# Attention and a routed expert layer in one kernel: the router's top logit carried in the row and applied after the expert gather, one table set per stage, a native fp32 router, shared-expert work inside the attention drain

## The chip, the cores and the metric

The kernel runs on one core of one Trainium2 chip. The metric is device time in microseconds (us) from launch to end. "Chunk" below is four row tiles of 128 tokens, 512 tokens; there are 32 tiles and 8 chunks. Engines: PE is TensorE (PEld its weight loads), DVE is VectorE, ACT ScalarE, POOL GpSimd, SP SyncE, which here only issues transfers.

## The reference

4096 tokens of 128 features pass through two residual blocks. Cut to what matters:

```python
def _L0_attn_ref(x, Wq, bq, Wk, bk, Wv, bv, Wo, bo, m):     # 16 heads of 8
    q = _l2norm(proj(Wq, bq)); k = _l2norm(proj(Wk, bk)); v = proj(Wv, bv)
    attn = jnp.einsum('bhid,bhjd->bhij', q, k) / n ** sigmoid(m)     # no softmax
    return jnp.einsum('bhij,bhjd->bhid', attn, v) ... @ Wo + bo

def _L0_ffn_ref(...):                                       # 16 experts, top 1
    logits = hidden @ router_w.T
    scores = sigmoid(top value, -inf elsewhere)
    routed_in = hidden[None, :, :] * scores.T[:, :, None]
    gate_up = einsum('nth,nhf->ntf', routed_in, gate_up_proj)
    routed_out = einsum('ntf,nfh->nth', up * silu(gate), down_proj)
    shared = silu(hidden @ shared_gate_w.T) * (hidden @ shared_up_w.T) @ shared_down_w.T

x = x + _L0_attn_ref(_layernorm(x), ...)
x = x + _L0_ffn_ref(_layernorm(x), ...)
```

## The kernel before

Each engine has one queue, and the order in it is the order in which the code is written for that engine; semaphores couple the five queues. There is no planner. Four stages follow one another.

**Attention.** Since there is no softmax, attention is q times (k'v), and `Wo` is folded into k'v. A loop over steps `s` works on several chunks at once. `project(s)` on PE makes q, k, v of chunk s; `take_qkv` on DVE scales and adds biases; `square` (ACT), `head_sums` (DVE), `head_norms` (ACT), `inv_norms` (DVE) and `scale_heads` (POOL) normalise the heads; `v_by_k`, `turn_q`, `fold_wo`, `attend` (PE) finish. `add_attn` (DVE, line 691) adds attention's output to the residual, `norm_h` (ACT) makes the second norm in `h_rows`, `turn_h` (PE) transposes it, `hT_hi` (ACT) and `hT_lo` (POOL) split it into two fp32r parts.

**Routing.** `route` multiplies with the router in three fp32r products per tile. `choose` (DVE) finds the expert of each token, `rank_tokens` (PE) counts, `place` (DVE) works out each token's row in a table `x_slots` in device memory, and `scatter` (POOL, line 397) writes the rows there by indirect transfers, 32 of them of 128 rows. Ahead of that, `score_rows` (ACT, lines 502 and 507) takes the sigmoid of the top logit and scales the row. After the last chunk SP fills the end of each expert's rows with zeros (16 transfers, line 300) and only then loads rows back.

**Windows.** 47 windows of 128 rows, in 12 groups of four, each window with the weights of one expert. `load_windows(q)` (SP, line 305) brings group q into `h_rows`; eight groups fit, so group q + 8 is loaded once group q's result has been stored:

```python
            for q in range(NG):
                sp.wait_ge(yg_rdy, q + 1)
                ...   # store yg
                if q + NQ < NG:
                    sp.wait_ge(gT_mm, q + 1)
                    load_windows(q + NQ)
```

`over_windows` sets the order on PE, ACT and DVE alike: in turn k `turn_x(k + 2)`, `gate_up(k)`, `turn_act(k - 1)`, `down(k - 2)`. On ACT these are `x_hi` (line 591), `silu_experts` (line 598), nothing, and `take_y` (line 608), which raises `yg_rdy`.

**Shared expert.** Chunks 0 and 1 (`gate_up_shared`, `down_shared`, lines 972 to 974 with `sgT`, `suT`, and 1009 to 1011) run before the windows, chunks 2 to 7 after them, beside 32 indirect gathers on POOL (line 424) that keep two transfers in flight.

Of the kernel before, what the change touches and what calls it, by code (L numbers as in the profile page):

```python
# [14 lines left out]
P = 128  # L15


def build_block(nc, x, xt, Wq, bq, Wk, bk, Wv, bv, Wo, bo, m, router_t, gate_up, down, gate_t, up_t, down_t, out):
# [16 lines left out]
    CAP = T + P  # L35
    QKV = 3 * D
# [6 lines left out]
    LATE = 2  # L43
# [3 lines left out]
    x_slots = nc.dram_tensor("x_slots", (E * CAP + SPARE * P, D), F32, kind="Internal").ap()  # L47
# [4 lines left out]
    with ExitStack() as ctx:  # L52
# [7 lines left out]
        h_rows = sb("h_rows", [P, NT, D])  # L60
# [17 lines left out]
        zero_rows = sb("zero_rows", [P, D])  # L78
        rwT = sb("rwT", [P, 2, E], F32R)
# [7 lines left out]
        top = sb("top", [P, NT])  # L87
        score = sb("score", [P, NT])
# [15 lines left out]
        win_no = sb("win_no", [1, NG * Q, E])  # L104
        win_start = sb("win_start", [1, NG * Q])
        past_n = sb("past_n", [1, NG * Q])
        past_jump = sb("past_jump", [1, NG * Q])
        win_e = sb("win_e", [1, NG * Q], I32)
        win_row = sb("win_row", [1, NG * Q], I32)
        gpos = sb("gpos", [P, NT], I32)  # L110

        with ExitStack() as attention:
            def sb_a(name, shape, dt=F32):
                return attention.enter_context(nc.sbuf_tensor(name, shape, dt))

# [28 lines left out]
        past = sb("past", [1, NG * Q, E])  # L144
        move = sb("move", [P, NT, E])
        moved = sb("moved", [P, NT])
        s_spl = sb("s_spl", [P, 2, 2, 512], F32R)
        yT = sb("yT", [P, 512])
        xgT = sb("xgT", [P, 2, 2, Q * P], F32R)
# [9 lines left out]
        ps_yT, ps_y = bank[0], bank[1]  # L159
        ps_gT, ps_aT, ps_yg = bank[3], bank[1], bank[2]  # L160
# [5 lines left out]
        ld_b, ld_wo, ld_wa = sem("ld_b"), sem("ld_wo"), sem("ld_wa")  # L166
# [11 lines left out]
        ssum, nrm, rn_rdy = sem("ssum"), sem("nrm"), sem("rn_rdy")  # L178
# [6 lines left out]
        top_rdy, log_read, score_rdy, hs_rdy = sem("top_rdy"), sem("log_read"), sem("score_rdy"), sem("hs_rdy")  # L185
        hot_rdy, rank_mm, rank_read, pos_rdy = sem("hot_rdy"), sem("rank_mm"), sem("rank_read"), sem("pos_rdy")
        scat = sem("scat")
# [4 lines left out]
        xg_ld = [sem(f"xg_ld{r}") for r in range(NQ)]  # L192
        gT_mm, gT_hi, gT_sb = sem("gT_mm"), sem("gT_hi"), sem("gT_sb")
# [11 lines left out]
        STEPS = NQ + 3  # L205
# [4 lines left out]

        def attended(s):

            return [c for c in range(NQ) if min(c + 3, NQ + 1) == s]

        def turned(s):

            return [c for c in range(NQ) if min(c + 4, NQ + 2) == s]

        def placed(s):

            return [c for c in range(NQ - LATE) if c + 5 == s]

        late = range(NQ - LATE, NQ)

# [4 lines left out]
        def rank_cols(c):  # L229

            at = ps_log[:, 256 + 80 * (c - late[0]):] if c in late else pair[:, 3, QKV:]
            return at[:, 0:(1 + Q) * E].rearrange("p (j e) -> p j e", e=E)
# [12 lines left out]
        def window_rows(q, engine):  # L245

            return table(win_row[0:1, Q * q:Q * q + Q], engine, E * CAP + (SPARE - 1) * P)

        def window_experts(q, engine):

            return table(win_e[0:1, Q * q:Q * q + Q], engine, (E - 1) * D)

        def over_windows(turn_x, gate_up, turn_act, down, filler):

            turn_x(0)
            turn_x(1)
            for k in range(NG + 2):
                if k + 2 < NG:
                    turn_x(k + 2)
                if k < NG:  # L260
                    gate_up(k)
                if 0 <= k - 1 < NG:
                    turn_act(k - 1)
                if 0 <= k - 2 < NG:
                    down(k - 2)
                if k >= NG:
                    filler(k - NG)
# [3 lines left out]
        def _(sp):  # L271
            for c in range(NQ):
# [6 lines left out]
                if c == 1:  # L279
                    sp.dma_start(bo_in[:], bo.partition_broadcast(2)).then_inc(ld_wo, 16)  # L280
# [13 lines left out]
            sp.dma_start(spare, zero_rows[:].unsqueeze(1).broadcast_to([P, SPARE, D])).then_inc(zero_st, 16)  # L294
# [7 lines left out]
            def load_windows(q):  # L302
                rows = window_rows(q, mybir.EngineType.SP)
# [6 lines left out]
            sp.wait_ge(scat, 16 * NT)  # L310
# [17 lines left out]
        def _(pool):  # L328
# [8 lines left out]
            g.memset(bo_pick[:, 1:2], 0.0)  # L337
            g.memset(zero_rows[:], 0.0).then_inc(k_set, 1)
# [20 lines left out]
            g.iota(base[:, 0, :], pattern=[[CAP, E]], base=0, channel_multiplier=0,  # L359
                   allow_small_or_imprecise_dtypes=True)  # L360
            g.iota(win_no[:], pattern=[[1, NG * Q], [0, E]], base=0, channel_multiplier=0,
                   allow_small_or_imprecise_dtypes=True)
            g.memset(hot[:, :, 0, :].bitcast(F32), 0.0)
            g.iota(win_start[:], pattern=[[P, NG * Q]], base=0, channel_multiplier=0,
                   allow_small_or_imprecise_dtypes=True).then_inc(k_ids, 1)

            def scale_heads(c, col, r_col, done):
# [3 lines left out]
                r = rn[:, c % 2, :, r_col:r_col + HEADS].unsqueeze(3).broadcast_to([P, Q, HEADS, HD])  # L371
# [13 lines left out]
            def weights_lo(n):  # L385
                w, raw = ((sgT, sg_in[:]), (suT, su_in[:]), (sdT, sd_in[:].rearrange("p k d -> p (k d)")),
                          (rwT, rw_in[:]))[n]
# [3 lines left out]
            def scatter(c, half):  # L391

                if half == 0:
                    pool.wait_ge(pos_rdy, c + 1)
                    pool.wait_ge(hs_rdy, c + 1)
# [754 lines left out]
```

## Time and profile before

| what | value |
|---|---|
| time, median of three runs | 272.96 us (272.4 to 273.98) |
| the profiled execution's own time | 275.04 us |
| its span | 273.3 us |
| mean granted TensorE clock | 0.845 |
| busy: PE, DVE, ACT, POOL | 219.1, 173.5, 135.7, 108.5 us |
| chain that ended last: PE, DVE, ACT, issue | 53%, 19%, 10%, 8% |

The span is what the trace covers; the run's time has 1.7 us more around it. Granted clock 1.00 is 2.4 GHz, 0.50 is 1.2 GHz; a value between is a mean over a stretch that saw both. Busy shares are averages over four stages with different limits.

### The profile page before, as it was taken

The page shows a single profiled execution, that of the slowest core. Times are in us where ns is not written, and L with a number is a line of the kernel's source. Part 1 is how long each engine was busy: PE and PEld are TensorE (multiplying, and loading weights), DVE is VectorE, ACT ScalarE, POOL GpSimd, SP SyncE. Part 2 cuts the span into 40 slices and gives each one's busy share as a digit, 9 for nine tenths or more (in the row PEclk, how much of TensorE's full clock was granted, in tenths as well). Part 3 has the DMA queues.
Part 4 walks back from the last instruction along what each step waited for, and adds up shares of the span by engine and source line. Part 5 has one row for each costly group of instructions (what it writes and reads, how often), then busy time and mean ns, then how long its engine had stood idle before and what let it go on. Part 6 is the DMA issues. An engine that isn't in the chain of part 4 may idle for free.

```text
span 273.3 us, 3732 instructions
## 1 busy us (share of the span) xinstructions
PE 219.1 (80%) x1059; PEld 171.0 (63%) x1059; DVE 173.5 (63%) x447; ACT 135.7 (50%) x265; POOL 108.5 (40%) x120
## 2 busy tenths in 40 slices
PE   0867598889898599299299556999999999999970
PEld 0325465666857488296278354888897677778740
DVE  2369899999978746245936424445546566776654
ACT  2424446758759878816135313444443556455630
POOL 6008466743756645474720000000000467675640
PEclk9995799897868755555569959999999999999998
DMA  5994238000100001001423330244123213222215
GB/s 147 319 336 151 77 116 260 1 0 1 39 13 29 19 26 35 19 29 40 149 73 104 109 97 0 67 136 121 56 79 116 59 31 86 77 47 79 77 38 154
DMA packets 33639, 23.32 MB, mean 85 GB/s; under 512 B 3154, under 2 KB 30804, under 8 KB 33620
## 3 DMA queue, kind: packets, MB, share of 16 engines
q1 hardware_dynamic: 30996, 18.69, 23.5%
q0 software_dynamic: 2048, 4.20, 5.4%
q10 hardware_dynamic: 576, 0.20, 0.3%
q8 instruction: 9, 0.15, 0.2%
q14 instruction: 10, 0.08, 0.1%
HBM read 13.77 MB, written 9.31 MB: 84 GB/s over the span
## 4 chain that ended last, share of the span: by engine, by line
PE 53%; DVE 19%; ACT 10%; issue 8%; POOL 4%; DMA 2%; ACTq 1%; DVEq 0%; POOLq 0%
PE quad_banks L972 9%; PE quad_banks L973 8%; PE quad_banks L974 8%; PE quad_banks L924 3%; PE bank L1009 3%; PE bank L1115 3%; PE bank L1088 3%; DVE qkv L663 3%; PE bank L1011 3%; PE bank L1010 3%; DVE ss L672 3%; DVE st L628 2%; ACT h_rows L452 2%; DMA w_qkv<-L_attn_Wv 2%; DVE xgT L854 2%
## 5 line engine op out<-in xcount | busy, mean ns | idle before, releaser
L424 POOL DMA_INDIRECT h_rows<-y_slots,gpos x32 | 32.7, 1022 | 92.4 <-DMA y_slots<-yg 75.6
L397 POOL DMA_INDIRECT x_slots<-h_rows,pos x32 | 31.6, 988 | 25.0 <-ACT h_rows L507 15.0
L740 DVE TENSOR_TENSOR s_act<-quad_banks,sg_act 128x512 f32<-128x512 f32 x32 | 22.0, 690 | 25.0 <-ACT sg_act L512 16.2
L512 ACT ACTIVATE sg_act<-quad_banks 128x512 f32<-128x512 f32 x32 | 19.1, 598 | 35.9 <-PE quad_banks L974 29.2
L924 PE MATMUL quad_banks<-w_c,xT 128*128 128x384 f32 x64 | 31.9, 661 | 0.6 <-issue 0.6
L372 POOL TENSOR_TENSOR qkv<-qkv,rn 128x512 f32<-128x512 f32 x16 | 16.9, 1074 | 32.5 <-DVE rn L680 32.5
L924 PEld LDWEIGHTS quad_banks<-w_c,xT 128*128 128x128 f32 x64 | 16.6, 272 | 13.3 <-issue 10.1
L854 DVE TENSOR_TENSOR xgT<-bank,xgT 128x512 fp32r<-128x512 f32 (+1 forms) x12 | 8.2, 680 | 25.8 <-ACT xgT L591 25.8
L518 ACT CAST s_spl<-s_act 128x512 fp32r<-128x512 f32 x32 | 19.6, 613 | 5.3 <-issue 4.8
L745 DVE TENSOR_TENSOR s_spl<-s_act,s_spl 128x512 fp32r<-128x512 f32 x32 | 21.9, 683 | 0.3
L591 ACT CAST xgT<-bank 128x512 fp32r<-128x512 f32 (+1 forms) x12 | 6.9, 576 | 27.5 <-PE quad_banks L974 23.3
L663 DVE SCALAR_TENSOR_TENSOR qkv<-quad_banks,rs,b_qkv 128x384 f32<-128x384 f32 x32 | 17.4, 598 | 3.8 <-PE quad_banks L924 3.8
L972 PE MATMUL quad_banks<-hT,sgT 128*128 128x512 f32 x32 | 14.2, 444 | 5.4 <-issue 5.4
L935 PE MATMUL bank<-qkv 128*128 128x128 f32 x64 | 11.0, 326 | 8.6 <-POOL qkv L372 8.6
L628 DVE BATCH_NORM_STATS2 st<-xres 128x6 f32<-128x128 f32 x64 | 13.8, 278 | 6.1 <-DMA xres<-L_attn_x 5.9
L1009 PE MATMUL bank<-s_spl,sdT 128*128 128x512 f32 x32 | 14.5, 454 | 3.2 <-DVE s_spl L745 3.2
L935 PEld LDWEIGHTS bank<-qkv 128*128 128x128 f32 x64 | 9.8, 234 | 10.2 <-POOL qkv L372 9.4
L972 PE MATMUL quad_banks<-w_gu,xgT 128*128 x47 | 15.0, 318 | 0.1
L452 ACT ACTIVATE h_rows<-xres,nm,rs 128x128 f32<-128x128 f32 x32 | 13.2, 482 | 2.4 <-DVE nm L649 2.0
L972 PE MATMUL bank<-rwT,hT 128*128 128x16 f32 x32 | 10.3, 321 | 5.1 <-POOL hT L376 4.8
L1088 PE MATMUL bank<-ident,h_rows 128*128 128x128 f32 x47 | 8.4, 306 | 7.3 <-DVE xgT L854 5.9
L973 PE MATMUL quad_banks<-w_gu,xgT 128*128 x47 | 13.8, 293 | 0.0
(161 smaller groups left out, 582.2 us busy)
## 6 DMA issues: line engine op xcount, KB each, us to landing
h_rows<-x_slots SPq DMA_DIRECT2D x47, 64.0 KB, 1.9
y_slots<-yg SPq DMA_DIRECT2D x11, 256.0 KB, 2.3
xT<-L_attn_x_turned SPq DMA_DIRECT2D x8, 256.0 KB, 6.1
xres<-L_attn_x SPq DMA_DIRECT2D x8, 256.0 KB, 6.1
w_raw<-L_ffn_gate_up_proj SPq DMA_DIRECT2D x4, 512.0 KB, 5.1
out<-xres SPq DMA_DIRECT2D x8, 256.0 KB
x_slots<-zero_rows SPq DMA_DIRECT2D x16, 64.0 KB
x_slots<-zero_rows SPq DMA_DIRECT2D x1, 960.0 KB, 9.8
```

What stands on the lines that cost most here:

```text
L397: g.indirect_dma_start(out=x_slots, out_offset=bass.IndirectOffsetOnAxis(ap=pos[:, t:t + 1], axis=0), in_=h_rows[:, t, :], in_offset=None) ...
L424: g.indirect_dma_start(out=h_rows[:, t, :], out_offset=None, in_=y_slots, in_offset=bass.IndirectOffsetOnAxis(ap=gpos[:, t:t + 1], axis=0) ...
L518: a.copy(s_spl[:, k % 2, 0], s_act[:, k % 2]).then_inc(s_hi, 1)
L663: last = v.scalar_tensor_tensor(out=qkv[:, c % QRING, j, :], in0=pair[:, j, 0:QKV], scalar=rs1[:, t:t + 1], in1=b_qkv[:], op0=ALU.mult, op ...
L740: v.tensor_tensor(s_act[:, k % 2], pair[:, 2 * (k % 2) + 1], sg_act[:, k % 2], ALU.mult).then_inc(s_act_rdy, 1)
L745: v.tensor_tensor(s_spl[:, k % 2, 1], s_act[:, k % 2], s_spl[:, k % 2, 0].bitcast(F32), ALU.subtract).then_inc(s_spl_rdy, 1)
L924: last = te.matmul(pair[:, j, 0:QKV], xT[:, at:at + P], w_c[:], start=True, stop=True)
L935: last = te.matmul(ps_vk[:, 0:D], qkv[:, c % QRING, j, 2 * D:QKV], qkv[:, c % QRING, j, D:2 * D], start=(h == 0 and j == 0), stop=(h == QB ...
L972: te.matmul(out, lhs[:, 0], rhs[:, 0], start=True, stop=False)
L973: te.matmul(out, lhs[:, 0], rhs[:, 1], start=False, stop=False)
L974: return te.matmul(out, lhs[:, 1], rhs[:, 0], start=False, stop=True)
L1009: te.matmul(ps_yT[:], w[:, 0], h[:, 0], start=(k == 0), stop=False)
```

## The change

- The residual's addition moves from DVE to PE: `attend` gains a product of the identity with `xres` (fp32, 512 columns), and ACT copies the sum (`take_x1`). `add_attn` goes.
- `head_sums` loses its maximum with 1e-24; POOL caps the reciprocals instead (`rn_cap`).
- `route` uses four fp32 products per chunk in place of twelve fp32r ones, and reads `hT_raw`. `rwT` and its split go.
- `choose` writes the top logit into a 129th column of `h_rows`; rows of `x_slots` are 132 numbers. `score_rows` goes. After a group is back in `h_rows`, ACT takes a tanh of its logits (`tanh_rows`), POOL makes the sigmoid of it and scales the rows (`scale_rows`). The built program has 3 ACT table loads.
- `place` reads rank and expert bases from PSUM and writes positions in one step; a running `tally` on DVE takes the place of `base`.
- `scatter` waits for the transfer but one before it.
- `split_bo` moves ahead of the attention loop on DVE; its load moves from SP to ACT's queue.
- Attention's last chunks are written out by hand, with `gate_up_shared(0, 0..2)` between them; expert tables are read per window (`of_windows`), on PE once a group; `xgT` has three buffers; the end of shared chunk 1 runs between the first windows.

```diff
-            def window_experts(q, engine):
-                return table(win_e[0:1, Q * q:Q * q + Q], engine, (E - 1) * D)
+            def of_windows(q, cells, engine, most):
+                return [table(cells[n:n + 1, 0:1], engine, most)[0] for n in windows(q)]
...
                 for t in tiles(c)[2 * half:2 * half + 2]:
+                    if t >= 2:
+                        pool.wait_ge(scat[t % 2], 16 * (t // 2))
                     g.indirect_dma_start(out=x_slots, ...
...
+            def scale_rows(q):
+                ...
+                pool.wait_ge(xg_tanh, q + 1)
+                g.tensor_scalar(score[:, r], squash[:, r], 0.5, 0.5, ALU.mult, ALU.add).then_inc(xg_score, 1)
+                pool.wait_ge(xg_score, q + 1)
+                g.tensor_tensor(rows, rows, score[:, r, 0:len(n)]..., ALU.mult).then_inc(xg_rdy, 1)
...
-            def score_rows(c):
-                a.activation(score[:, t], top[:, t], ACT.Sigmoid).then_inc(score_rdy, 1)
-                ...
-                    last = a.activation(row, row, ACT.Copy, scale=score[:, n:n + 1])
...
+            def take_x1(c):
+                act.wait_ge(y_mm, c + 1)
+                a.copy(xres[:, Q * c:Q * c + Q, :], ps_qy[:]...).then_inc(x1_rdy, 1)
...
+            def tanh_rows(q):
+                r = q % NQ
+                n = len(windows(q))
+                act.wait_ge(xg_ld[r], 16 * (n + Q * (q // NQ)))
+                if q >= NQ:
+                    act.wait_ge(xg_rdy, q - NQ + 1)
+                a.activation(squash[:, r, 0:n], h_rows[:, Q * r:Q * r + n, D], ACT.Tanh, scale=0.5).then_inc(xg_tanh, 1)
...
+            def x_hi_and_tanh(q):
+                if q == 0:
+                    tanh_rows(0)
+                    tanh_rows(1)
+                    tanh_rows(2)
+                x_hi(q)
+                if q + 3 < NG:
+                    tanh_rows(q + 3)
...
-                v.tensor_tensor(r, ps_qy[:]..., r, ALU.add).then_inc(x1_rdy, 1)
-                v.tensor_scalar(ss[:, c % 2], ss[:, c % 2], 1e-24, None, ALU.max).then_inc(ssum, 1)
...
-                link(v.tensor_tensor(here[:], here[:], hot[:, c, 1:1 + Q, :].bitcast(F32), ALU.mult))
-                link(v.tensor_reduce(pos_f[:, t], here[:], AX.X, ALU.add))
-                v.tensor_copy(pos[:, t], pos_f[:, t]).then_inc(pos_rdy, 1)
+                v.tensor_tensor(here[:], rank[:, 0:Q, :], hot[:, c, 1:1 + Q, :].bitcast(F32), ALU.mult
+                                ).then_inc(rank_read, 1)
+                dve.wait_ge(rank_read, c + 1)
+                v.tensor_reduce(pos[:, t], here[:], AX.X, ALU.max).then_inc(pos_rdy, 1)
...
+                te.matmul(ps_qy[:], ident[:], xres[:, Q * c:Q * c + Q, :].rearrange("p j d -> p (j d)"),
+                          start=False, stop=True).then_inc(y_mm, 1)
...
-                    last = split_product(ps_log[:, at:at + E], hT[:, :, P * t:P * t + P], rwT)
+                    last = te.matmul(ps_log[:, at:at + E], hT_raw[:, c % 2, P * j:P * j + P], rw_in[:],
+                                     start=True, stop=True)
```

ACT's queue at the loading of the ninth group. Before, two turns of the windows (`xgT` rows are `x_hi`, `eg_act` rows `silu_experts`, `yg` rows `take_y`):

```order
L598 ACTIVATE eg_act<-quad_banks 128x512
L608 COPY yg<-bank 128x512
L591 CAST xgT<-bank 128x512
L598 ACTIVATE eg_act<-quad_banks 128x512
L608 COPY yg<-bank 128x512
```

And now, turns 2 to 4; `squash` rows are `tanh_rows` of groups 7, 8 and 9, and `xg_ld` is raised by the landing of a group's rows:

```order
L610 ACTIVATE squash<-h_rows 128x4 [waits xg_ld7]
L624 ACTIVATE eg_act<-quad_banks 128x512 [waits e_act_rdy,e_gu_mm]
L634 COPY yg<-bank1 128x512 [waits e_dn_mm]
L617 CAST xgT<-bank3 128x512 [waits e_gu_mm,gT_mm]
L610 ACTIVATE squash<-h_rows 128x4 [waits xg_rdy,xg_ld0]
L624 ACTIVATE eg_act<-quad_banks 128x512 [waits e_act_rdy,e_gu_mm]
L634 COPY yg<-bank1 128x512 [waits e_dn_mm]
L617 CAST xgT<-bank3 128x512 [waits e_gu_mm,gT_mm]
L610 ACTIVATE squash<-h_rows 128x4 [waits xg_rdy,xg_ld1]
```

A row that waits for a transfer now stands between `take_y(0)` and `silu_experts(3)`, and one like it in each of the three turns after.

POOL's queue behind the last head scaling. Before (`x_slots` rows are scatters, `hT` rows `hT_lo`):

```order
L397 DMA x_slots<-h_rows,pos 69504x128 [waits hs_rdy,pos_rdy]
L397 DMA x_slots<-h_rows,pos 69504x128
L376 TENSOR_TENSOR hT<-hT_raw,hT 128x512 [waits hT_hi_rdy] x2
L397 DMA x_slots<-h_rows,pos 69504x128 x2
L397 DMA x_slots<-h_rows,pos 69504x128 [waits hs_rdy,pos_rdy]
L397 DMA x_slots<-h_rows,pos 69504x128 x3
```

Now, the last chunk's scatters and what follows them:

```order
L385 DMA x_slots<-h_rows,pos 69504x132 [waits scat0,pos_rdy]
L385 DMA x_slots<-h_rows,pos 69504x132 [waits scat1]
L385 DMA x_slots<-h_rows,pos 69504x132 [waits scat0]
L385 DMA x_slots<-h_rows,pos 69504x132 [waits scat1]
L364 TENSOR_TENSOR hT<-hT_raw,hT 128x512 [waits hT_hi_rdy] x2
L393 TENSOR_SCALAR score<-squash 128x4 [waits xg_tanh]
L395 TENSOR_TENSOR h_rows<-h_rows,score 128x4x128 [waits xg_score]
```

Each scatter waits for the landing of the one two before it, and two rows for each group of windows stand behind the scatters.

## Rows read from the trace of the kernel before

**Rows 1.** Stretches: us, busy us (count) per engine, granted clock, DMA share, GB/s.
```profile
68.00:80.00 12.00, 11.09 (x52) 8.09 (x50) 10.18 (x32) 8.87 (x19) 7.87 (x8) 0.72 0.07 23
...
96.00:121.84 25.84, 20.15 (x88) 18.41 (x88) 11.26 (x44) 16.83 (x38) 14.06 (x15) 0.50 0.08 26
...
156.30:212.00 55.70, 48.54 (x342) 42.62 (x343) 25.55 (x49) 20.53 (x37) 0.00 (x0) 0.94 0.30 84
```

**Rows 2.** Timeline of DVE and POOL (start, us): `split_bo`, and `place` of two chunks.
```profile
24.53 2.95 DVE L702 SCALAR_TENSOR_TENSOR bo_r<-bo_hi,bo_pick,bo_part 2x512 fp32r<-2x512 f32 x1
...
64.96 2.11 POOL L372 TENSOR_TENSOR qkv<-qkv,rn 128x512 f32<-128x512 f32 x2 [3.58 <-DVE rn L680]
65.08 1.03 DVE L731 TENSOR_TENSOR here<-here,hot 128x64 f32<-128x64 f32 x1
...
95.68 0.22 DVE L731 TENSOR_TENSOR here<-here,hot 128x64 f32<-128x64 f32 x1
```

**Rows 3.** Groups by line: xcount, busy us, mean ns, idle before.
```profile
L502 ACT ACT_TABLE_LOAD x5 | 6.4, 1283 | 0.1
...
L691 DVE TENSOR_TENSOR xres<-bank,xres 128x512 f32<-128x512 f32 x8 | 5.5, 682 | 1.5 <-PE bank L966 1.5
L376 POOL TENSOR_TENSOR hT<-hT_raw,hT 128x512 fp32r<-128x512 f32 x8 | 10.1, 1273 | 3.9 <-ACT hT L462 3.8
...
L972 PE MATMUL quad_banks<-hT,sgT 128*128 128x512 f32 x32 | 14.2, 444 | 5.4 <-issue 5.4
...
L676 DVE TENSOR_SCALAR ss<-ss 128x128 f32<-128x128 f32 x8 | 3.7, 463 | 0.3
```

**Rows 4.** Timeline of PE: `project(4)`, the last `project`, the last `rank_tokens`.
```profile
42.04 2.75 PE L924 MATMUL quad_banks<-w_c,xT 128*128 128x384 f32 x8
...
74.69 5.18 PE L924 MATMUL quad_banks<-w_c,xT 128*128 128x384 f32 x8
...
125.94 0.79 PE L993 MATMUL bank<-hot,ones_r 128*128 128x48 f32 x3
```

**Rows 5.** Timeline of POOL: two scatters in a row, first and last of 32 gathers.
```profile
119.17 0.96 POOL L397 DMA_INDIRECT x_slots<-h_rows,pos  x1 [0.30 <-issue]
120.43 0.95 POOL L397 DMA_INDIRECT x_slots<-h_rows,pos  x1 [0.30 <-issue]
...
213.97 0.98 POOL L424 DMA_INDIRECT h_rows<-y_slots,gpos  x1 [75.63 <-DMA y_slots<-yg]
...
262.54 0.94 POOL L424 DMA_INDIRECT h_rows<-y_slots,gpos  x1 [0.33 <-issue]
```

**Rows 6.** SP's queue (zero fills, loads), its table reads, and DVE's `pad_row`.
```profile
129.73 11.04 SPq L300 DMA_DIRECT2D x_slots<-zero_rows  x16
142.61 19.19 SPq L305 DMA_DIRECT2D h_rows<-x_slots  x32
...
L240 SPq TENSOR_LOAD <-win_row x12: 296/301/314, 142.1 to 186.4; - x12
...
128.69 0.32 DVE L793 CAST pad_row<-base 1x16 int32<-1x16 f32 x1
```

**Rows 7.** Windows: SP's stores and loads, `take_y` between, the loads' landing.
```profile
178.21 0.38 SPq L317 DMA_DIRECT2D y_slots<-yg  x1
...
181.47 0.59 ACT L608 COPY yg<-bank 128x512 f32<-128x512 f32 x1 [0.28 <-PE bank L1115]
...
182.09 0.38 SPq L317 DMA_DIRECT2D y_slots<-yg  x1
...
182.99 1.88 SPq L305 DMA_DIRECT2D h_rows<-x_slots  x4
...
DMA to landing us min/median/max: 1.7/1.9/2.0
```

**Rows 8.** Timeline of PE: first product of the first and of the last group.
```profile
161.79 0.57 PE L972 MATMUL quad_banks<-w_gu,xgT 128*128 x1
...
203.54 0.38 PE L972 MATMUL quad_banks<-w_gu,xgT 128*128 x1
```

More of the change, by code:

```diff
@@ L309, in _ @@
             sp.wait_ge(pad_st, 16 * E)
-            sp.wait_ge(scat, 16 * NT)
+            for landed in scat:
+                sp.wait_ge(landed, 16 * NT // 2)
             for q in range(NQ):
@@ L413, in _ @@
                     split_lo(SPLIT_STEPS.index(s))
-            for c in (late[0] - 1, *late):
+            scatter(3, 0)
+            hT_lo(5)
+            scatter(3, 1)
+            for c in range(4, NQ):
                 scatter(c, 0)
                 scatter(c, 1)
+            hT_lo(6)
+            hT_lo(7)
+            for q in range(NG):
+                scale_rows(q)
             pool.wait_ge(gpos_rdy, 1)
@@ L530, in _ @@
             std(rs1, mv1, var1, std1, 0)
-            for s in range(STEPS):
-                if live(s + 1):
-                    std(rs1, mv1, var1, std1, s + 1)
-                for c in turned(s):
-                    hT_hi(c)
-                if 1 <= s < 5:
+            std(rs1, mv1, var1, std1, 1)
+            for s in range(NQ):
+                if live(s - 3):
+                    take_x1(s - 3)
+                if live(s - 4):
+                    take_hT(s - 4)
+                square(s)
+                if live(s - 1):
+                    qT_copy(s - 1)
+                if live(s - 4):
+                    hT_hi(s - 4)
+                if live(s - 3):
+                    std(rs2, mv2, var2, std2, s - 3)
+                head_norms(s)
+                if live(s - 3):
+                    norm_h(s - 3)
+                if live(s + 2):
+                    std(rs1, mv1, var1, std1, s + 2)
+                if live(s - 1) and (s - 1) % 2:
+                    wb_copy((s - 1) // 2)
+                if 1 <= s < 4:
                     weights_hi(s - 1)
@@ L608, in take_y, with lead @@
                 a.copy(yg[:, q % YRING, 0:n], ps_yg[:].rearrange("p (j d) -> p j d", d=D)[:, 0:n]).then_inc(yg_rdy, 1)
+            def x_hi_and_tanh(q):
[6 more added lines that the diff above has]
+                    tanh_rows(q + 3)
+            def lead(k):
+                if k == 1:
+                    yT_copy(C1 - 1)
             shared(0, C1)
-            over_windows(x_hi, silu_experts, nothing, take_y, lambda k: silu_shared(C1, k))
+            hi_shared(C1 - 1, KC - 1)
+            over_windows(x_hi_and_tanh, silu_experts, nothing, take_y, lead, lambda k: silu_shared(C1, k))
             shared(C1, NQ)
+            end_shared(NQ)
         @block.vector
@@ L753, in _ @@
             v.reciprocal(m_tmp[:, 2:3], m_tmp[:, 1:2]).then_inc(m_step, 1)
+            split_bo()
             x_stats(1)
             x_scales(0)
-            for s in range(STEPS):
-                if live(s):
-                    take_qkv(s)
+            for s in range(NQ):
+                take_qkv(s)
                 if s == 0:
@@ L784, in _ @@
-                for c in placed(s):
-                    place(c)
-            v.engine_nop().then_inc(y_free, 1)
-            for c in late:
-                choose(c)
-            for c in late:
-                place(c)
-            v.tensor_copy(pad_row[:], base[0:1, NQ, :]).then_inc(pad_rdy, 1)
-            link(v.scalar_tensor_tensor(out=tot_i[:], in0=base[:, NQ, :], scalar=float(P - 1), in1=base[:, 0, :],
-                                        op0=ALU.add, op1=ALU.subtract))
+                inv_norms(s)
@@ new lines, in _ @@
+            choose(3)
+            mask_vk(3)
+            x1_stats(5)
+            place(3)
+            h_scales(5)
+            choose(4)
+            x1_stats(6)
+            place(4)
+            h_scales(6)
+            x1_stats(7)
+            choose(5)
+            h_scales(7)
+            choose(6)
+            place(5)
+            act_shared(0, 0)
+            place(6)
+            choose(7)
+            act_shared(0, 1)
+            place(7)
+            total = rank_cols(NQ - 1)[:, Q, :]
@@ L991, in rank_tokens @@
                 te.matmul(rank[:, 0:Q, :], before_r[:], mine[:, 1:1 + Q, :], start=False, stop=False)
-                for s in range(2, Q + 1):
-                    last = te.matmul(rank[:, s:1 + Q, :], ones_r[:], mine[:, 1:2 + Q - s, :], start=False, stop=(s == Q))
+                for s in range(1, Q + 1):
+                    last = te.matmul(rank[:, s:1 + Q, :], ones_r[:], mine[:, 0:1 + Q - s, :], start=False, stop=(s == Q))
                 last.then_inc(rank_mm, 1)
```

429 lines of the change are left out of this document (234 added, 195 removed).

## The prediction, made before the changed kernel was run

> **What bounds the kernel now.** I read first the busy time by stretches. TensorE is the busiest engine in every stage, but never at its limit. Before the routing it works 11.1 of 12.0 us at a granted clock of 0.72; in the drain of the attention stage 20.2 of 25.8 us at 0.50, its lower level, 1.2 GHz; in the windows 48.5 of 55.7 us [rows 1]. So a stage's end is set by chains, and I read those from the timelines.
>
> Three moments cut the program. The last `project` ends at 74.69 + 5.18 = 79.9 us and the last `rank_tokens` at 125.94 + 0.79 = 126.7 us [rows 4]. SP's zero fills start at 129.73 and last 11.0 us; about 1.3 us later they have landed and SP goes on, at 142.1 us, the first read of `win_row` [rows 6]. Call this W. The first load follows at 142.61 [rows 6]. The first product of the windows starts at 161.8 us, the first of the last group at 203.5 [rows 8], and from there to the end of the span, 273.3, are 69.8 us. W to end is thus 131.2 us. What a change is worth can be read from how it moves the last `project` (79.9), W less that (62.2), and the end less W (131.2).
>
> **Up to the last project.** `split_bo` stood among the attention steps with one instruction of 2.95 us [rows 2]; now it stands where DVE waits for the second chunk's rows. That is worth about 3. Each step loses on DVE the residual's addition (0.68) and the maximum (0.46) [rows 3]. Multiplying `here` took 0.22 us once and 1.03 us while POOL scaled heads [rows 2]; it now reads PSUM, and its two companions go, about 1.2 in the last three steps, less some 0.5 for the tally, bounded by rows of this size (0.22). That is 1.1 in the two middle steps and 1.8 in three, 7.6 in all. The table loads, 1.28 each, five at line 502 and five alike at line 446 [rows 3], go from ACT, which was not the bound of a step. Against it PE gets 512 fp32 columns: 384 of them take 2.75 / 4 = 0.69 us at the full clock [rows 4], so 0.92, and about 1.8 at the lower one; the cheaper router gives back less than half of that. PE would bind at 9 to 10 us a step. The sum lies between -3 + 5 x 0.92 = +1.6 (all of it on the path) and -3 - 7.6 = -10.6; I take **-6**, nearer to the saved end because DVE, not PE, stood in the way in most steps. The last project ends at 74.
>
> The Trainium skill, "SBUF — State Buffer", section "SBUF: two separate sides", says that DVE with two SBUF inputs and a POOL instruction that reads SBUF lock each other out for a whole instruction. The row of 1.03 agrees. By that rule the new POOL multiplication in the windows is free for DVE, whose instructions there read PSUM; no row before has POOL busy there.
>
> **From the last project to W.** Two chains end here. The routing chain took 126.7 - 79.9 = 46.8 us. Six of the table loads lay in it (6 x 1.28 = 7.7), and PE's 20.2 busy us there ran at 0.50; with shared work between them I expect the full clock for about half, worth 5. Two more shared units come in, 12 products of at most 0.44 [rows 3], and three of the new additions, 0.92 each: 8.1 in all, of which I let 5.7 go into the gaps that PE had there [rows 1]. 46.8 - 7.7 - 5 + 8.1 - 5.7 is 36.5, say 37. Then 2.0 for `place` and `pad_row`, less than the 129.0 - 126.7 = 2.3 of now [rows 4, 6], the fills 11.0 and 1.3: 51 us after the last project.
>
> The other chain is POOL's. After the last project it still has the scatters of chunks 1 to 7, 28 of them. Now a scatter starts 120.43 - 119.17 = 1.26 us after the one before, without waiting for any landing; the gathers, which keep two in flight as the scatters will, come every (262.54 - 213.97) / 31 = 1.57 us [rows 5]. I take the gathers' pace: 44.0. With two pairs of head scalings (2.11 each [rows 2], and a cap of some 0.4) 5.0, three `hT_lo` of 1.27 [rows 3] 3.8, and 2.0 for the last landing it comes to 54.8. With 1.26 it would be 46, and the fills would decide at 51. So W is 55 after the last project where it was 62.2: **-7**. W comes at 74 + 55 = 129.
>
> **From W to the end.** Here I see something that the change pays for. In the windows ACT now carries `tanh_rows(k + 5)` in turn k, between `x_hi(k + 2)` and `silu_experts(k)`, and it waits for a transfer. Group q + 8 is loaded only after `take_y(q)`, which is the last thing in turn q + 2. So `tanh_rows(8)` in turn 3 waits for a load that was let go at the end of turn 2, and behind it in ACT's queue stand `silu_experts(3)` and `take_y(1)`, which lets the next load go. Before, nobody needed group 8 until PE's `turn_x(8)` in turn 6. The loop for turns 3 to 6 is: `take_y` ends at 181.47 + 0.59 = 182.06, the first load is issued at 182.99, 0.93 later, and the last of four 1.55 after it (1.88 less its own 0.33); it lands 1.9 later [rows 7]. A table read takes 0.30 [rows 6] and there are four instead of one: 0.9 more. Then tanh, 0.2, and two ACT passes like `take_y`, 0.6 each. That is 0.93 + 0.9 + 1.55 + 1.9 + 0.2 + 1.2 = **6.7 us** where a turn takes 182.09 - 178.21 = 3.9 now [rows 7]. Three turns cost 6.7 and the one with three windows 5.9.
>
> The start: eight groups of loads take 19.19 us [rows 6], 2.4 a group, and 3.3 with the three further reads. ACT's tanh of group 7 comes before `silu_experts(2)` and `take_y(0)`, so the first `take_y` ends at W + 26.6 + 1.5 (landing, from the last issue's start) + 1.4 = W + 29.6. PE is done with the shared chunks by then and idles. The loop takes it to W + 29.6 + 26.0 = 55.6; `gate_up_experts(8)` starts 2.5 later, at 58.1; three turns of 3.9 bring `gate_up_experts(11)` to 69.8; and the tail is unchanged, 69.8. W to end is 139.6 where it was 131.2: **+8.4**.
>
> The Trainium skill, "Runtime: NRT & Kernel Launch", section "Instruction fetch mechanics", gives a register load about 200 ns per register even for several at once. By that page one read of four registers and four reads of one cost the same 0.8. The trace has 0.30 for four [rows 6], so it doesn't bear the page out; by the page the loop would be 0.9 shorter, and as an estimate the whole some 5 us shorter.
>
> **Sum.** -6 - 7.2 + 8.4 = -4.8 on the span of 273.3: 268.5. The profiled execution's own 275.04 would be 270.2, and against the median, 272.96, which is 2.1 below the profiled run, **268.2 us**.
>
> **Rivals.**
> - *The landing is hidden* (15%). If ACT has time to spare in each turn and the wait costs nothing, the loop is at 3.9: 11 us less, **257 us**. ACT's 20.5 busy of 55.7 us [rows 1] speak for it; against it, slack doesn't help a wait for something that is let go only one instruction earlier.
> - *PE eats the gain of the attention stage* (13%). If the added fp32 product is on the path and the clock stays mixed, the last project ends at 80, all else as above: **274 us**, no change. For it speaks 11.1 of 12.0 us at 0.72 [rows 1].
> - *Slower: the scatters* (17%). They are now paced by their landing, write rows of 528 bytes, and nothing of this was measured before. All of W hangs on 28 of them. The balance is at a pace of 1.57 + 4.8 / 28 = 1.74 us; at 1.9, the landing of a load [rows 7], W comes 9 us later: **277 us**.
> - The likeliest (55%): 268, its own range 263 to 273, for the register reads (0.9 in each of 12 loads, 5 us the one way) and the last project at 70 to 78.
>
> **Numbers.** A measurement of this kernel can tell about 0.5%, 1.4 us. Faster by more: 0.15 for the first rival and 0.51 of the likeliest, 0.66. Within: the 0.13 of the second less 0.01, and 0.04 of the likeliest, 0.16. Slower: the 0.17 of the third and that 0.01, 0.18. The range that leaves out 2 in 10 is 258 to 277, from next to the first rival to the last.
>
> **What would show it.** ACT's tanh instructions of groups 8 to 11 with 3 us and more of idle time ahead of each, released by the loads into `h_rows`, and turns of 6 to 7 us there; POOL without a gap from the last project to the last scatter, at 1.5 to 1.6 us apiece; the zero fills over before the last scatter has landed; PE idle before the first window. The last `project` should end near 74. The prediction is wrong if the windows' turns keep 3.9 us, if scatters come slower than 1.74, or if the last project ends after 79.

## The result, and the profile after

The changed kernel takes 280.32 us (median; 279.28 to 282.13), the kernel before 272.98 beside it: a ratio of 1.0296, 95% interval 1.0229 to 1.0362, so 3% slower. I had forecast 268.2, within 258 to 277. The profiled execution has a span of 279.3 us where it was 273.3. These lines of its page answer to the figures of before:

```profile
span 279.3 us, 3768 instructions
PE 213.1 (76%) x1051; PEld 168.2 (60%) x1051; DVE 157.9 (57%) x422; ACT 116.4 (42%) x235; POOL 125.2 (45%) x151
PE 43%; SPq 11%; DMA 10%; ACT 9%; DVE 8%; issue 8%; POOL 8%; ACTq 1%; DVEq 0%; POOLq 0%
L991 PE MATMUL bank<-qkv 128*128 128x128 f32 x64 | 12.0, 348 | 17.5 <-POOL qkv L360 17.5
L610 ACT ACTIVATE squash<-h_rows 128x4 f32<-128x4 f32 (+1 forms) x12 | 2.5, 208 | 41.5 <-DMA h_rows<-x_slots 41.5
```

ACT and DVE do less than before, as meant, and yet the span grew. The last two lines say where to look: PE stands 17.5 us ahead of `v_by_k` (L991), waiting for POOL's scaled heads, and ACT stands 41.5 us ahead of its twelve tanh instructions, waiting for loads.

The three moments of the prediction, in the timelines of the changed kernel (start, length): the last `project` on PE, the last `rank_tokens`, SP's zero fills, its loads, and the first product of `gate_up_experts(8)` and `(11)`:

```profile
78.52 2.75 PE L980 MATMUL quad_banks<-w_c,xT 128*128 128x384 f32 x8
121.98 0.59 PE L1063 MATMUL bank<-hot,ones_r 128*128 128x64 f32 x4
123.89 10.92 SPq L284 DMA_DIRECT2D x_slots<-zero_rows  x16
139.62 25.48 SPq L289 DMA_DIRECT2D h_rows<-x_slots  x32
199.81 0.38 PE L1030 MATMUL quad_banks<-w_gu,xgT 128*128 x1 [0.45 <-issue]
209.77 0.38 PE L1030 MATMUL quad_banks<-w_gu,xgT 128*128 x1
```

W, SP's first read of `win_row`, is the first start in this row (count, ns minimum/median/maximum, first and last start in us), beside it PE's reads of `win_e`:

```profile
L225 SPq TENSOR_LOAD <-win_row x47: 264/278/642, 138.3 to 191.5; - x47
L225 PEldq TENSOR_LOAD <-win_e x47: 301/310/488, 154.5 to 209.2; - x47
```

| us | before [rows 4, 6] | forecast | after |
|---|---|---|---|
| last `project` ends | 79.9 | 74 | 81.3 |
| from there to W | 62.2 | 55 | 57.0 |
| W to the end | 131.2 | 139.6 | 141.0 |
| span | 273.3 | 268.5 | 279.3 |

The second and third lines went as forecast to 2.0 and 1.4 us. The first was to gain 6 and lost 1.4: of the 10.8 us that the forecast of the span is off, 7.3 stand there. A last `project` after 79 was one of the prediction's own signs of being wrong.

**What held the attention steps.** The chain of waits (start, length, what ran, of the work that ended last) shows the same four POOL instructions in each of the steps 1 to 3, and in step 4 the last three of them. One such turn:

```profile
47.33 1.65 ACT h_rows L458 x4
49.17 0.52 ACT sdT L508
49.75 1.28 POOL sdT L376
51.03 2.33 POOL w_gu L370
53.37 0.50 POOL rn L358
53.94 1.08 POOL qkv L360
```

`sdT` and `w_gu` are the splits of weights into two fp32r parts (`weights_hi` and `split_hi` on ACT, `weights_lo` and `split_lo` on POOL), which attention doesn't need. DVE's part of the next chunk was done before them:

```profile
48.47 0.92 DVE L718 RECIPROCAL rn<-rn 128x128 f32<-128x128 f32 x1
```

It was done at 49.39, but POOL took its cap of `rn` up at 53.32 only. Before, ACT split ahead of `square(s)`; POOL's splits were over (44.6) before DVE's `rn` came (47.1), and POOL then waited 2.54 us for it:

```profile
42.25 2.34 POOL L382 TENSOR_TENSOR w_gu<-w_raw,w_gu 128x1024 fp32r<-128x1024 f32 x1
47.13 2.11 POOL L372 TENSOR_TENSOR qkv<-qkv,rn 128x512 f32<-128x512 f32 x2 [2.54 <-DVE rn L680]
```

The change moved ACT's two splits behind everything else in the step. POOL, whose own order is unchanged, waits for them with the next scaling behind it.

**What held the windows.** ACT's tanh of groups 8 and 9, and what follows each in ACT's queue:

```profile
173.76 0.21 ACT L610 ACTIVATE squash<-h_rows 128x4 f32<-128x4 f32 x1 [5.46 <-DMA h_rows<-x_slots]
173.88 0.58 ACT L624 ACTIVATE eg_act<-quad_banks 128x512 f32<-128x512 f32 x1
174.35 0.58 ACT L634 COPY yg<-bank 128x512 f32<-128x512 f32 x1
180.76 0.21 ACT L610 ACTIVATE squash<-h_rows 128x4 f32<-128x4 f32 x1 [5.34 <-DMA h_rows<-x_slots]
```

That is the loop of the prediction: tanh, silu, `take_y`, store and load, tanh. `take_y(0)` starts at 167.23, the next four at 174.35, 181.35, 189.76 and 195.83: turns of 7.1, 7.0, 8.4 and 6.1 us. The third is the longest because its last load took 3.36 us to land where that of the turn before took 1.95; the chain of waits has both (why, no run here shows):

```profile
178.79 1.95 DMA h_rows<-x_slots
185.79 3.36 DMA h_rows<-x_slots
```

### The profile page after: what moved, and what is told of

The parts are those of the page before. It is cut to its first block, busy times and chain, and to the rows that moved or that the text cites. A ratio compares the mean times of both kernels' runs of the same rounds, so it can differ in the third digit from the quotient of the medians.

```text
span 279.3 us, 3768 instructions
## 1 busy us (share of the span) xinstructions
PE 213.1 (76%) x1051; PEld 168.2 (60%) x1051; DVE 157.9 (57%) x422; ACT 116.4 (42%) x235; POOL 125.2 (45%) x151
## 4 chain that ended last, share of the span: by engine, by line
PE 43%; SPq 11%; DMA 10%; ACT 9%; DVE 8%; issue 8%; POOL 8%; ACTq 1%; DVEq 0%; POOLq 0%
SPq L289 6%; PE quad_banks L1030 6%; PE quad_banks L1031 5%; PE quad_banks L1032 5%; DMA x_slots<-h_rows,pos 5%; SPq L225 5%; PE quad_banks L980 4%; POOL w_gu L370 3%; DMA h_rows<-x_slots 3%; PE bank L991 3%; ACT h_rows L458 3%; PE bank L1081 3%; PE bank L1083 2%; PE bank L1082 2%; DMA w_qkv<-L_attn_Wv 2%
## 5 line engine op out<-in xcount | busy, mean ns | idle before, releaser
L980 PE MATMUL quad_banks<-w_c,xT 128*128 128x384 f32 x64 | 26.3, 565 | 0.6 <-issue 0.6
L914 DVE TENSOR_TENSOR e_act<-quad_banks,eg_act 128x512 f32<-128x512 f32 (+1 forms) x12 | 8.2, 680 | 32.8 <-ACT eg_act L624 32.8
L991 PE MATMUL bank<-qkv 128*128 128x128 f32 x64 | 12.0, 348 | 17.5 <-POOL qkv L360 17.5
L785 DVE TENSOR_TENSOR s_spl<-s_act,s_spl 128x512 fp32r<-128x512 f32 x32 | 24.0, 750 | 0.2
L991 PEld LDWEIGHTS bank<-qkv 128*128 128x128 f32 x64 | 10.7, 253 | 20.0 <-POOL qkv L360 14.0
L393 POOL TENSOR_SCALAR score<-squash 128x4 f32<-128x4 f32 x12 | 2.3, 193 | 41.7 <-ACT squash L610 41.7
L980 PEld LDWEIGHTS quad_banks<-w_c,xT 128*128 128x128 f32 x64 | 14.1, 232 | 10.5 <-issue 5.7
L610 ACT ACTIVATE squash<-h_rows 128x4 f32<-128x4 f32 (+1 forms) x12 | 2.5, 208 | 41.5 <-DMA h_rows<-x_slots 41.5
L1030 PE MATMUL quad_banks<-w_gu,xgT 128*128 x47 | 16.1, 343 | 3.0 <-issue 2.3
L1179 PE MATMUL bank<-ident,h_rows 128*128 128x128 f32 x47 | 10.0, 350 | 8.4 <-DVE xgT L906 6.2
L1211 PE MATMUL bank<-w_dn,e_actT 128*128 x94 | 15.0, 311 | 0.0
```

The source lines that it names most:

```text
L785: v.tensor_tensor(s_spl[:, k % 2, 1], s_act[:, k % 2], s_spl[:, k % 2, 0].bitcast(F32), ALU.subtract).then_inc(s_spl_rdy, 1)
L980: last = te.matmul(pair[:, j, 0:QKV], xT[:, at:at + P], w_c[:], start=True, stop=True)
L991: last = te.matmul(ps_vk[:, 0:D], qkv[:, c % QRING, j, 2 * D:QKV], qkv[:, c % QRING, j, D:2 * D], start=(h == 0 and j == 0), stop=(h == QB ...
L1030: te.matmul(out, lhs[:, 0], rhs[:, 0], start=True, stop=False)
```

## Experiments

Each is named by its label; "the changed kernel" is their base unless another is given. All compute the full reference.

**e1_splits.** Four lines moved within ACT's step:

```
+                if 1 <= s < 4:
+                    weights_hi(s - 1)
+                if s in SPLIT_STEPS:
+                    split_hi(SPLIT_STEPS.index(s))
                 square(s)
...
-                if 1 <= s < 4:
-                    weights_hi(s - 1)
-                if s in SPLIT_STEPS:
-                    split_hi(SPLIT_STEPS.index(s))
```

> The changed kernel, with ACT's splits of the weights (weights_hi, split_hi) back ahead of square(s) in each step, where the kernel before had them. Theory: in the changed kernel POOL reaches the next chunk's cap and scaling only at 53.32 us, though DVE's rn was ready at 49.39, since in its queue weights_lo and split_lo wait for ACT, which splits last in its step. That is 3.9 us in one step and there are four such steps; part of it will be given to the next limit (DVE's step). Last project from 81.3 to between 72 and 75, the rest of the program unchanged, so about 272 us (270 to 275) where the changed kernel takes 280.3. Rival: the attention steps are held by PE (the added fp32 product, the low clock): last project moves by less than 1 us, time 279 to 281.

Measured 269.92 us, ratio to the kernel before 0.9891 (0.9821 to 0.996): 10.4 below the changed kernel, and 1.1% below the kernel before. POOL and the last `project` in its timeline, and W:

```profile
41.11 2.38 POOL L370 TENSOR_TENSOR w_gu<-w_raw,w_gu 128x1024 fp32r<-128x1024 f32 x1
45.70 0.53 POOL L358 TENSOR_SCALAR rn<-rn 128x128 f32<-128x128 f32 x1 [2.21 <-DVE rn L718]
68.02 2.75 PE L980 MATMUL quad_banks<-w_c,xT 128*128 128x384 f32 x8
L225 SPq TENSOR_LOAD <-win_row x47: 267/277/640, 127.1 to 180.6; - x47
```

In the step shown, POOL is done with its splits 2.2 us before `rn` comes, as in the kernel before. The last project ends at 70.8, W is 56.3 later, and from W to the end it is 141.3: only the first stage moved, by 10.5.

**e4_before_splits_last.** The opposite edit in the kernel before: in steps 1 to 3 the same splits put last on ACT (the change moved those of step 4 too).

> The kernel before, with ACT's splits of the weights in steps 1 to 3 put last in the step, where the change put them. Theory: POOL waits for them ahead of the next chunk's scaling also here: last project from 79.9 to between 83 and 88, time 276 to 281 where the kernel before takes 273.0. Rival: their place doesn't matter, and what the changed kernel loses in the attention steps is due to the residual's product or the cap on POOL: 272 to 274.

Measured 277.15 us, ratio 1.0131 (1.0039 to 1.0224). The wait appears here too:

```profile
46.22 1.28 POOL L389 TENSOR_TENSOR sdT<-sd_in,sdT 128x512 fp32r<-128x512 f32 x1 [5.06 <-ACT sdT L496]
49.78 2.10 POOL L372 TENSOR_TENSOR qkv<-qkv,rn 128x512 f32<-128x512 f32 x2
76.57 5.32 PE L926 MATMUL quad_banks<-w_c,xT 128*128 128x384 f32 x8
```

The last project ends at 81.9, 2.0 later than before, which is less than I expected (83 to 88), and the profile accounts for only 1.6 us of span (274.9). A difference of 2.0 in this moment is no more than single profiles of one arrangement spread (see e5), so the sign rests on the times, whose interval lies above 1, and on the wait of 5.06 us itself. The size is smaller than in the changed kernel: three steps and not four were moved, and what else makes it smaller isn't shown.

**e2_late_tanh.** The tanh of groups 8 to 11 taken out of `x_hi_and_tanh` and put ahead of `take_y`, as `tanh_rows(k + 3)` in turn k:

```
-                if q + 3 < NG:
+                if q + 3 < NQ:
                     tanh_rows(q + 3)
+            def late_tanh(q):
+                if NQ <= q + 4 < NG:
+                    tanh_rows(q + 4)
...
-            over_windows(x_hi_and_tanh, silu_experts, nothing, take_y,
+            over_windows(x_hi_and_tanh, silu_experts, late_tanh, take_y,
```

> The changed kernel, with tanh_rows(8) to (11) two turns later on ACT, each just ahead of take_y of its turn and five turns after the groups loaded first, nothing else moved. Theory: the four turns of 7.0, 7.0, 8.4 and 6.1 us are a loop through ACT's wait for a load that take_y let go one instruction earlier; without that wait they cost 3.4 to 3.9 each, 13 us less in all: 267 us (265 to 270), and no idle time over 1 us ahead of the tanh of groups 8 to 11. Rival: the turns are held by what SP does for each group (store, four table reads, four loads, 2.3 + 1.6 + 1.9 us), or by PE's table reads, so that the wait comes back at turn_x: less than 4 us gained, 276 us or more.

Measured 279.2 us, ratio 1.0236 (1.0165 to 1.0306): 1 us gained where I expected 13. (Its profile, of the quickest of its four executions, has 3.9 us less from W to the end.) The wait for the load is gone, but see what follows the tanh of group 8 (ACT, POOL, PE):

```profile
177.40 0.60 ACT L624 ACTIVATE eg_act<-quad_banks 128x512 f32<-128x512 f32 x1 [1.68 <-PE quad_banks L1036]
177.89 0.20 ACT L610 ACTIVATE squash<-h_rows 128x4 f32<-128x4 f32 x1
178.45 1.04 POOL L395 TENSOR_TENSOR h_rows<-h_rows,score 128x512 f32<-128x512 f32 x1
179.55 0.66 PE L1183 MATMUL bank<-ident,h_rows 128*128 128x128 f32 x4 [0.86 <-POOL h_rows L395]
181.29 0.38 PE L1034 MATMUL quad_banks<-w_gu,xgT 128*128 x1 [1.08 <-issue]
183.87 0.60 ACT L624 ACTIVATE eg_act<-quad_banks 128x512 f32<-128x512 f32 x1 [3.04 <-PE quad_banks L1036]
```

On PE `turn_x(k + 3)` stands ahead of `gate_up_experts(k + 1)`. So silu, tanh, POOL's scaling, `turn_x`, `gate_up_experts` and the next silu are a ring of their own, 183.87 - 177.40 = 6.5 us in this turn and 5.6 to 5.9 in the next ones. The edit was a turn too late. The rival named the right size, under 4 us, but not this ring, so neither of my theories was right.

**e2b_tanh_one_turn_later and e5_tanh_in_time.** In both, `tanh_rows(k + 4)` stands right behind `silu_experts(k)`; in e2b for groups 8 to 11 alone (its condition is `NQ <= q + 4 < NG`), in e5 for all, with `x_hi(0)` behind the first two tanh:

```
+            def silu_and_tanh(q):
+                silu_experts(q)
+                if q + 4 < NG:
+                    tanh_rows(q + 4)
```

> The changed kernel, with the tanh of groups 8 to 11 alone moved one turn later on ACT: tanh_rows(k + 4) behind silu_experts(k) where it was tanh_rows(k + 5) ahead of it. The start of the windows is as in the changed kernel. Theory: the four turns of 7.0, 7.0, 8.4 and 6.1 become 3.4 to 3.9 each, 13 us less: 267 us (265 to 270). Rival, SP's chain holds the turns: 274 to 277.

> The changed kernel, with tanh_rows(k + 4) right behind silu_experts(k) in turn k for every group, and x_hi(0) behind the tanh of groups 0 and 1 alone. The run with tanh_rows(k + 3) there gained only 1 us: the idle time ahead of the tanh was gone, but it ran through tanh, POOL's scaling (1.3 us), turn_x(k + 3), gate_up_experts(k + 1) and silu_experts(k + 1) in turns of 5.7 us. Theory now: a group needs both, its tanh a turn ahead of turn_x and two turns behind the take_y that lets its load go; then turns are 3.4 to 3.9 and four of them 13 us cheaper, and since take_y(0) no longer waits for the load of group 7, it ends some 8 us sooner than W + 29.5. 262 us (258 to 266). Rival: what holds the turns is SP's chain of store, four reads and four loads, 4.2 us a group and more; then no more than 6 us are gained in all: 274.

Measured 267.07 us (ratio 0.9787, 0.97 to 0.9873) and 267.83 us (0.9807, 0.9734 to 0.9879). ACT in e2b, tanh of groups 8 and 9, and W in e2b and e5:

```profile
172.57 0.21 ACT L610 ACTIVATE squash<-h_rows 128x4 f32<-128x4 f32 x1
176.88 0.21 ACT L610 ACTIVATE squash<-h_rows 128x4 f32<-128x4 f32 x1 [0.48 <-DMA h_rows<-x_slots]
L225 SPq TENSOR_LOAD <-win_row x47: 266/278/650, 137.0 to 182.0; - x47
```

```profile
L225 SPq TENSOR_LOAD <-win_row x47: 265/277/649, 140.5 to 182.4; - x47
```

From W to the end e2b takes 265.7 - 137.0 = 128.7 us, 12.3 less than the changed kernel: the loop's price. e5 takes 266.3 - 140.5 = 125.8, another 2.9 less and not the 8 expected. There SP is the limit, as the rival had it, though not at its price: `take_y(0)` is done at 166.9, but SP is busy with the first eight groups' loads, at 3.2 us a group, until 167.8, and from then its stores follow one another every 4.2 us (167.89, 172.11, 176.30), with four reads and four loads between. In its times that gain doesn't show. Its last project ends at 82.0 where e2b's, with the same instructions, ends at 80.1: this moment lies between 78.2 and 82.0 in the profiles of six kernels whose attention steps are alike, so single profiles are compared stage by stage here.

**e3_row_tables.** The window tables along one partition again, and one read for four cells:

```
-            return [table(cells[n:n + 1, 0:1], engine, most)[0] for n in windows(q)]
+            return table(cells[0:1, Q * q:Q * q + len(windows(q))], engine, most)
```

> The changed kernel, with the windows' experts and first rows written along one partition as in the kernel before, so that one read fetches the four of a group, on SP and on PE. Theory: a read of one cell and a read of four both take about 0.3 us, so a group's loads need 2.4 us instead of 3.2. Eight groups: 6.4 us earlier at the last load of group 7, which ACT's tanh waits for ahead of the first take_y; the loop of four turns 0.8 each: 3.2. About 271 us (269 to 274). Rival: a read costs by the register, so that four at once take as long as four apart: no change, 279 to 281.

Measured 270.84 us, ratio 0.9982 (0.9903 to 1.0062): 9.5 below the changed kernel. SP's loads of eight groups, and its reads:

```profile
137.11 18.64 SPq L290 DMA_DIRECT2D h_rows<-x_slots  x32
L226 SPq TENSOR_LOAD <-win_row x12: 295/302/924, 136.6 to 180.3; - x12
```

A read of four cells has a median of 302 ns, a read of one 278. The eight groups take 18.6 us and not 25.5, and W to the end is 268.0 - 136.6 = 131.4, 9.6 less. That the expected 6.4 + 3.2 = 9.6 came out is in part luck: the first `take_y` ends 3.7 us sooner after W, since it now waits for PE and not for a load, and the four turns after it are 4.1 shorter.

**e6_unpaced and e8_all_unpaced.** Scatters that wait for no landing, in the changed kernel and in e7_all:

```
-                    if t >= 2:
-                        pool.wait_ge(scat[t % 2], 16 * (t // 2))
```

> The changed kernel, with scatters that wait for no earlier landing (one semaphore, awaited in full by SP, as in the kernel before). Theory: the last 20 scatters come 1.49 us apart and last land at 138.2 us, 2 us behind the zero fills; unpaced they are issued 1.26 apart, so that the fills decide and W comes some 2 us earlier: 278 us (277 to 280). Rival: the pacing costs more than that, since it also holds hT_lo behind it in POOL's queue: 275 or less. Other rival: unpaced scatters land later, no change, 280.

> e7_all with the unpaced scatters of e6_unpaced. Theory: unpaced, the time from the last project to SP's first read of win_row was 53.8 us against 57.0 (the fills decide), and here the last scatter is what decides as well: 2 to 3 us less than e7_all's 249.5, about 247. Rival: with the last project 10 us sooner the scatters are released by pos and not by landings, so that the pace matters less: 249 to 250.

e6: 277.54 us (ratio 1.0189, 1.0128 to 1.0251). From the last project (80.5) to W (134.3) it is 53.8 us where it was 57.0. So the pacing costs about 3 us. e8, however, takes 257.3 us (0.9412, 0.9347 to 0.9476), 8 us more than e7_all (below) and against both theories. In its timeline, DVE and ACT during the burst of scatters:

```profile
111.55 0.23 DVE L773 TENSOR_TENSOR here<-bank,hot 128x64 f32<-128x64 f32 x1 [4.44 <-remote]
117.91 0.23 DVE L752 TENSOR_REDUCE h_rows<-bank 128x4 f32<-128x64 f32 x1 [5.89 <-remote]
119.39 0.60 ACT L512 ACTIVATE sg_act<-quad_banks 128x512 f32<-128x512 f32 x1 [9.83 <-remote]
```

What they compute on was ready before: `rank_tokens(6)` ended at 108.0, `route(7)` at 110.5, the gate and up products of the shared chunk at 113.2. With inputs ready they stood 3.5, 5.9 and 6.2 us. POOL meanwhile issued 14 scatters 1.26 us apart, from 99 to 117 us; the first wait ended within that burst, the other two when it had paused. The burst alone isn't the reason: in e6, POOL issued 18 in a row at the same pace, from 107 to 130 us, and after each wait of over 1 us DVE and ACT went on within 0.1 us of the end of what they waited for. The profile names no releaser, and why they stood stays open. e8 comes to W 62.2 us after the last project, 4.9 later than e7_all, and the shared work left over brings the first product of the windows 19.3 us after W instead of 14.3.

**e7_all.** e1, e3 and e5 together:

> The changed kernel with three edits together: ACT's splits ahead of square(s) as in e1_splits (10 us there), four table cells to a read as in e3_row_tables (9.5 us there), and the tanh of each group right behind silu_experts four groups earlier as in e5_tanh_in_time. Theory: the last project at 71, W 57 after it, and from W to the end 11 us to the first gate_up_experts, eleven turns of 3.4 and a tail of 69.5: 71 + 57 + 11 + 37 + 70 = 246 us of span, 248 us of time (244 to 253), 25 below the kernel before. Rival: the edits overlap, since the row reads took most of their gain from the same loop of load and tanh, and PE at 3.9 us a turn and the loads at 2.4 us a group bind: 254 to 260.

Measured 249.48 us, ratio 0.9172 (0.9103 to 0.924): 8% faster than the kernel before.

```profile
67.86 2.75 PE L985 MATMUL quad_banks<-w_c,xT 128*128 128x384 f32 x8
L226 SPq TENSOR_LOAD <-win_row x12: 295/301/923, 127.9 to 162.4; - x12
145.20:184.00 38.80, 38.27 (x319) 37.36 (x318) 24.75 (x47) 20.21 (x42) 9.69 (x16) 1.00 0.41 111
```

The last row is a stretch of the windows (length, then busy us of PE, PEld, DVE, ACT and POOL, and the granted clock): PE works 38.3 of 38.8 us at the full clock. The three stages are 70.6, 57.3 and 118.2; 10.4 + 9.5 + 12.5 = 32.4 us were to be gained by the single runs, and 30.8 were.

**e9, e10, e11: single terms of the attention steps**, each undone in e7_all: the residual added by DVE, the cap of `rn` on DVE, `split_bo` in step 1. In e9 `attend` ends without the product with `ident`, and

```
             def x1_stats(c):
-                dve.wait_ge(x1_rdy, c + 1)
+                dve.wait_ge(y_mm, c + 1)
+                r = xres[:, Q * c:Q * c + Q, :]
+                v.tensor_tensor(r, ps_qy[:].rearrange("p (j d) -> p j d", d=D), r, ALU.add).then_inc(x1_rdy, 1)
+                dve.wait_ge(x1_rdy, c + 1)
```

> e7_all with the residual added by DVE again (x1_stats adds ps_qy to xres; no product with ident in attend, no take_x1 on ACT). It tells whether the product's 0.92 us of PE a step, or DVE's 0.68, is on the path of the attention steps. Theory of the prediction: DVE stands in the way in most steps, PE in few, so the last project comes 1 to 4 us later than 70.6: time 251 to 253. Rival: PE is as much on the path; the last project comes as early or earlier, and six products less of the routing chain: 246 to 249.5.

> e7_all with the cap of rn behind the reciprocal on DVE and not on POOL. POOL's cap takes 0.53 us and 0.6 from its start to the scaling's, and it lies in series with the scaling; DVE's would lie in series too (the kernel before had 0.46 for the maximum), so the last project moves by less than 2 us: 248 to 251.5. Rival: POOL's queue was so full that half a us a step there is 4 us in all: 246.

> e7_all with split_bo back in step 1, behind take_qkv(1), where the kernel before had it. Theory of the prediction: its instruction of 2.95 us stood on the path there, so that the last project comes 3 us later, 252 to 253. Rival: it lies beside a wait of DVE's for PE or POOL in that step, 249 to 250.

e9: 252.9 us (0.9269, 0.9219 to 0.9318), 3.4 slower than e7_all; their executions don't overlap (252.4 to 254.4 against 247.9 to 251.4), the two intervals just do. Its last project and that of e11, which took 249.87 us (0.9167, 0.9097 to 0.9238), no difference:

```profile
71.64 2.75 PE L987 MATMUL quad_banks<-w_c,xT 128*128 128x384 f32 x8
```

```profile
69.86 2.75 PE L986 MATMUL quad_banks<-w_c,xT 128*128 128x384 f32 x8
```

They end at 74.4 and 72.6, against 70.4 to 71.0 in the four other profiles with the splits in place (e1, e7, e8, e10). In e9 the chain of waits from 49 to 74 us runs through DVE alone, and the residual's addition is on it in each of three steps, 0.6 us each. (The granted clock from 22 to 68 us is 0.86 in e9 and 0.93 in e7_all; PE isn't on that chain.) e10's four executions took 244.95 to 255.14 us, the quickest at a granted clock of 0.93 and the others at 0.88 to 0.89, so its times say nothing of the cap. Its profile, at the same clock as that of e7_all, has:

```profile
67.64 2.75 PE L984 MATMUL quad_banks<-w_c,xT 128*128 128x384 f32 x8
```

The last project ends at 70.4 against 70.6: in this one profile the place of the cap makes no difference.

## Why the prediction was wrong

**Up to the last project, -6: the step that failed.** Of the terms that I counted, two were tested alone: the residual has the sign that I gave it, and `split_bo` shows no difference in the times. The maximum and `here` were not tested. With the splits back in their place the stage ends at 70.8, 9.1 before the old one and 3 more than I took. "DVE, not PE, stood in the way" holds: taking the residual off DVE and onto PE, in spite of its fp32 product, is worth 3.4 us (e9). The rival that PE eats the gain is out as the cause, though 81.3 lies near its 80: e1 has the same product on PE and ends at 70.8. But `split_bo` was worth 0.4 us in the times and at most 2.0 in the profile, not 3. What failed is that I summed over what was added and removed and left out what was only moved; so even my bounds, -10.6 to +1.6, which hold the measured +1.4, hold it by luck. The splits on ACT cost the same wherever they stand; behind the norms they came 4 us late for POOL, and the next scaling waited behind POOL's half of them. That cost 10.5 us of the stage (e1; 7 to 11 if each of the six profiles named under e5 is taken instead of this one), and the opposite edit makes the kernel before slower (e4). The reason I gave for the table loads, that ACT was not the bound of a step, was true of its busy time and hid what its order does.

**To W, -7.2: right, measured -5.2.** The scatters decide, as forecast: the fills are issued by 134.8 us, the last scatter at 135.88 with a landing of 2.3. The backlog's last eighteen, with nothing else between them, start (135.88 - 109.86) / 17 = 1.53 us apart, for which I had 1.57. The chain is 57.0 and not 54.8; what I had left out is that POOL also stands for `hT_hi` (1.69 and 2.67 us ahead of two `hT_lo`). The routing chain took 41.3 us and not 37, and wasn't the later one; its granted clock was 0.79 (seventh figure of this row, busy us of PE, PEld, DVE, ACT and POOL ahead of it) against the 0.75 that "the full clock for about half" means:

```profile
81.30:122.60 41.30, 36.58 (x191) 30.01 (x190) 25.44 (x100) 22.25 (x49) 29.14 (x30) 0.79 0.10 34
```

The slower rival needed a pace of 1.74; it didn't come.

**From W to the end, +8.4: right, measured +9.8.** The first `take_y` ends at W + 29.5 (forecast 29.6). The turns are 7.1, 7.0, 8.4 and 6.1 where I had three of 6.7 and one of 5.9. From the end of `take_y` to the first load it is 170.13 - 167.81 = 2.32 us, forecast 0.93 + 0.9, because the four reads take up to 0.6 us each there. So `gate_up_experts(8)` came 3.4 us later after W than forecast (61.5 for 58.1); three turns of 3.3 us where I took 3.9 gave 1.7 back, and the tail is 69.5. So the agreement to 1.4 us is in part two misses that cancel. The wait of ACT is 12.3 of it (e2b) and the reads by single cell are 9.6 (e3), in part the same microseconds. The rival "the landing is hidden" is out.

**The table reads.** The page of the Trainium skill that the prediction weighed, "Runtime: NRT & Kernel Launch", section "Instruction fetch mechanics", gives about 200 ns for each register. The trace disagrees, 302 ns for four and 278 for one, and it decides. I had this in the sum, 3 x 0.3 us a group on SP, at the right size for the first eight groups (3.2 us a group, forecast 3.3). PE's four reads of 0.31 a group, 1.2 us where two reads of the kernel before took 0.7, I hadn't counted.

## What to carry to other kernels

Cost what a change moves like what it adds: for each moved instruction, find who waits for its semaphore and what stands behind that wait in the waiter's queue. An instruction that waits for a transfer belongs, in an in-order engine, behind everything that lets the transfer go, and far enough ahead of its own reader that it doesn't open a second ring; one turn made the difference between 1 us and 13 (e2, e2b). A change that is slower as a whole may hold good parts: with three moves mended, this one is 8% faster.

## What was unexpected of the hardware

A read of four table cells into registers took 302 ns, of one cell 278 (medians, SP), so four single reads cost over three times one joint read. Two engines whose inputs were ready stood for 3.5 to 6.2 us beside a burst of 14 scatters of POOL 1.26 us apart (e8), and did not beside a longer one in e6; the cause is open. And the granted clock can differ between executions of one kernel, 0.93 against 0.88, with 245 against 252 to 255 us (e10).
